# A two-stage recurrent and routed layer on one Trainium2 core: a new order of work at the changeover between its stages

## The reference

```python
xn = _layernorm(x, axis=-1)
s = recurrence(xn, A, BC)      # h = h * A + xn_t over the 2048 steps of a sequence, then h @ BC
scores = einsum('bsh,eh->bse', xn, gate_w)          # 8 experts
chosen = argmax(scores, axis=-1)
y = xn + einsum('bsh,fh->bsf', xn, expert_w[chosen])  # each token: the expert with the top score
g = silu(y)
x = x + s * g
```

## Time and profile before

| | |
|---|---|
| median of 3 runs | 529.57 us (529.09 to 530.28) |
| the profiled execution, its own time | 528.31 us |
| its span | 526.6 us |
| TensorE (matmul) busy in the span | 498.6 us, 95% |
| VectorE busy | 415.2 us, 79% |
| GpSimd busy | 317.9 us, 60% |
| ScalarE busy | 260.3 us, 49% |
| HBM traffic | 235 GB/s over the span |

### The profile page before, as it was taken

How to read it: one execution, slowest core, us unless ns; L and a number is a source line. 1 busy time by engine, 2 the same in 40 slices (tenths; PEclk the granted TensorE clock), 3 DMA queues, 4 the chain that set the end, 5 groups by cost and what they waited for, 6 DMA issues and landing times. The chain is left out here.

```text
span 526.6 us, 10784 instructions
## 1 busy us (share of the span) xinstructions
PE 498.6 (95%) x2776; PEld 391.8 (74%) x2777; DVE 415.2 (79%) x1068; ACT 260.3 (49%) x500; POOL 317.9 (60%) x358
## 2 busy tenths in 40 slices
PE   6699999999999999999987999999999999999993
PEld 6466776777777777777776888888888888887882
DVE  5979899899989998999732677777777777777773
ACT  4556676677677667767720333333333333333330
POOL 3535756766766676666644366666766666656652
PEclk9989999999999999999988999999999999999998
DMA  8995777887877787787346467776867777757720
GB/s 235 383 344 159 249 218 237 254 229 249 263 238 235 240 260 217 249 266 239 114 124 203 138 222 240 230 250 217 268 224 228 227 234 214 228 193 249 228 80 10
DMA packets 65411, 116.98 MB, mean 222 GB/s; under 512 B 8842, under 2 KB 26250, under 8 KB 65300
## 3 DMA queue, kind: packets, MB, share of 16 engines
q1 hardware_dynamic: 47328, 64.59, 39.2%
q0 software_dynamic: 18048, 52.02, 31.3%
HBM read 66.27 MB, written 57.48 MB: 235 GB/s over the span
## 5 line engine op out<-in xcount | busy, mean ns | idle before, releaser
L983 PE MATMUL ps_s<-w_hi,split 128*128 x284 | 118.8, 418 | 0.1
L596 ACT ACTIVATE ps_s<-ps_s 128x512 f32<-128x512 f32 x71 | 41.3, 582 | 154.5 <-issue 94.5
L470 POOL DMA_INDIRECT out_dram<-work x71 | 73.7, 1038 | 71.8 <-issue 45.3
L984 PE MATMUL ps_s<-w_lo,split 128*128 x284 | 112.9, 398 | 0.0
L985 PE MATMUL ps_s<-w_hi,split 128*128 x284 | 112.8, 397 | 0.0
L902 PE MATMUL ps_s<-bc_hi,split 128*128 128x512 f32 x256 | 105.3, 411 | 0.0
L903 PE MATMUL ps_s<-bc_lo,split 128*128 128x512 f32 x256 | 102.4, 400 | 0.0
L460 POOL DMA_INDIRECT work<-token_rows,work x71 | 72.6, 1023 | 31.1 <-issue 24.4
L394 POOL TENSOR_TENSOR split<-work,split 128x1024 fp32r<-128x1024 f32 x32 | 76.2, 2380 | 10.1 <-ACT split L524 9.9
L412 POOL DMA_INDIRECT slot_table<-token_id,slot_id x64 | 63.0, 985 | 26.1 <-issue 20.9
L638 DVE TENSOR_TENSOR_SCAN work<-a_col,work,ps_xt 128x256 f32<-128x256 f32 x112 | 74.3, 725 | 0.2
(11 more groups left out here) (103 smaller groups left out, 734.1 us busy)
## 6 DMA issues: line engine op xcount, KB each, us to landing
token_rows<-work SPq DMA_DIRECT2D x31, 528.0 KB, 3.1
work<-in_L_attn_inputs_dram SPq DMA_DIRECT2D x31, 512.0 KB
token_rows<-work SPq DMA_DIRECT2D x29, 512.0 KB
work<-in_L_ffn_expert_w_dram SPq DMA_DIRECT2D x128, 64.0 KB
slot_table<-w_lo SPq DMA_DIRECT2D x1, 4160.0 KB, 17.8
token_rows<-in_L_attn_inputs_dram SPq DMA_DIRECT2D x3, 512.0 KB
work<-token_rows,work POOLq DMA_INDIRECT x71
out_dram<-work POOLq DMA_INDIRECT x71
```

Of the source, the lines that this page charges most:

```text
L470: nc.gpsimd.indirect_dma_start(out=out_flat, out_offset=bass.IndirectOffsetOnAxis(ap=slot_tok[:, n:n + 1], axis=0), in_=o_sb[:, u], in_off ...
L983: nc.tensor.matmul(z_ps[v], hi, wh, start=(k == 0), stop=False)
L984: nc.tensor.matmul(z_ps[v], hi, wl, start=False, stop=False)
```

## The change

FIRST = 3 is new. What it does, by engine:

- **GpSimd.** Its last two groups are written out in another order: the id scatters of group 30 go ahead of `low_part` of group 31. Once all ids have landed it reads, in three small indirect DMAs (128 lines of 64 bytes each, `first_ids`), the ids of the first three tiles straight into `ids2`. It gathers the rows of tile 0 by them, and only then reads the whole table (`all_ids`), then gathers tiles 1 and 2 by `ids2`, and tiles 3 to 5 by `slot_tok`. The iota for `j_row` moves to the start of the kernel, with two more (`j_first`, `slot_first`).
- **TensorE.** In group 30 the ranks stand between the two `product_hi`, and `score_parts` of group 31 waits for the slots of group 30. The counts are made directly behind the ranks of group 31, by two more products with its one-hot rows, so they don't wait for GpSimd's last `seen` (whose last sum is gone). The 34 + 46 transposes are gone; 26 products of 128x512 with a block of weights (`stay_busy`) stand there, their results unused. The transpose of the ids of all tiles stands inside the products of tile 0, after the ninth of twelve. Tile 1 is turned after tile 0's products, no longer before them.
- **VectorE.** It places group 30 before it routes group 31, reads the counts between the two steps of placing group 31, and computes the slots of three tiles (`slot2`) ahead of `blk_row`. In stage 2, `low_x2` of tile 0 stands directly behind its `normalise`, then the conversion of the table, `normalise` of tile 1, the copy to `slot_tok`, `low_x2` of tile 1, `normalise` of tile 2.
- The little buffers of the plan lie in `xnt`, no longer in `work`. SyncE and ScalarE keep their order.

The diff, cut to its core:

```diff
@@ gpsimd
-            for c in range(GROUPS):
+            for c in range(GROUPS - 2):
                 group(0, c, left=GROUPS - 1 - c)
-            nc.gpsimd.iota(j_row, ...)
+            count(0, GROUPS - 2)
+            next_ids(0, GROUPS - 1)
+            scatter_ids(0, GROUPS - 2)
+            low_part(0, GROUPS - 1)
+            scatter_ids(0, GROUPS - 1)
+
             for v in range(2):
                 pool.wait_ge(id_stored[v], 32 * (GROUPS // 2))
-            pool.wait_ge(blk_row_ready, 1)
-            nc.gpsimd.indirect_dma_start(
-                out=blk_i[0:PLANNED].rearrange("p q w -> p (q w)"), out_offset=None, in_=table,
...
+            def first_ids(j):
+                pool.wait_ge(slot2_ready, 1)
+                nc.gpsimd.indirect_dma_start(
+                    out=ids2[:, j], out_offset=None, in_=table_flat,
+                    in_offset=bass.IndirectOffsetOnAxis(ap=slot2[:, j:j + 1], axis=0),
+                    bounds_check=TROWS * P - 1, oob_is_err=False).then_inc(ids2_loaded[j], 16)
+
+            def all_ids():
+                pool.wait_ge(blk_row_ready, 1)
+                pool.wait_ge(lo_done, GROUPS)
...
             def gather(it, c):
...
-                pool.wait_ge(slot_tok_ready, 1)
-                wait(pool, o_ready, n - RR + 1)
+                if n < FIRST:
+                    pool.wait_ge(ids2_loaded[n], 16)
+                    tok = ids2[:, n, 0:1]
+                else:
+                    pool.wait_ge(slot_tok_ready, 1)
+                    wait(pool, o_ready, n - RR + 1)
+                    tok = slot_tok[:, n:n + 1]
...
+            for j in range(FIRST):
+                first_ids(j)
             for v in range(2):
                 pool.wait_ge(s_stored[v], 16 * (GROUPS // 2 + (TPG - 1 if v == LAST else 0)))
-            for c in range(RR):
+            gather(0, 0)
+            all_ids()
+            for c in range(1, RR):
                 gather(0, c)
@@ vector
+                if left == 1:
+                    place(it, c, 0)
+                    place(it, c, 1)
                 if left == 0:
                     place(it, c, 0)
+                    nc.vector.tensor_scalar(tile_i[:, 0], count_ps, float(P - 1), None, ALU.add).then_inc(plan_step, 1)
                     place(it, c, 1)
...
             normalise(0, 0)
+            low_x2(0, 0)
+            dve.wait_ge(blk_loaded, 16)
+            nc.vector.tensor_copy(blk_f[0:PLANNED], blk_i[0:PLANNED, :, 0]).then_inc(blk_f_ready, 1)
             normalise(0, 1)
-            low_x2(0, 0)
+            dve.wait_ge(slot_turned, 1)
+            nc.vector.tensor_copy(slot_tok[:, :], slot_ps[:, 0:TILES]).then_inc(slot_tok_ready, 1)
+            low_x2(0, 1)
             normalise(0, 2)
-            low_x2(0, 1)
@@ tensor
+            turn_x(0, GROUPS - 1)
+            product_hi(0, GROUPS - 2, 0)
+            ranks(0, GROUPS - 2)
+            product_hi(0, GROUPS - 2, 1)
+            score_parts(0, GROUPS - 1, placed=True)
+            product_lo(0, GROUPS - 2, 0)
+            product_lo(0, GROUPS - 2, 1)
+            scores(0, GROUPS - 1)
+            ranks(0, GROUPS - 1, counted=True)
             product_hi(0, GROUPS - 1, 0)
-            pe.wait_ge(seen_ready, GROUPS)
-            pe.wait_ge(slot_ready, GROUPS)
...
             product_lo(0, GROUPS - 1, 0)
             product_hi(0, GROUPS - 1, 1)
             product_lo(0, GROUPS - 1, 1)
-            keep_warm(x2_ps[0], 34)
-            pe.wait_ge(blk_f_ready, 1)
-            nc.tensor.transpose(slot_ps[:, 0:PLANNED], blk_f[0:PLANNED], ident[0:PLANNED, 0:PLANNED]).then_inc(slot_turned, 1)
-            keep_warm(x2_ps[0], 46)
+            def stay_busy(times):
+
+                for _ in range(times):
+                    nc.tensor.matmul(x2_ps[1], w_hi[:, 0, 0:P], w_hi[:, 0], start=True, stop=True)
+
+            stay_busy(26)
...
+                    if isinstance(it, int) and it + c == 0 and k == CH - 2:
+                        turn_slots()
...
             turn_x2(0, 0)
-            for c in range(RR):
+            tile(0, 0, ahead=False)
+            turn_x2(0, 1)
+            for c in range(1, RR):
                 tile(0, c)
```

More of the change, by code:

```diff
@@ L205, in bass_recurrent_routed @@
         blk_loaded = sem("blk_loaded")
+        ids2_loaded = [sem(f"ids2_loaded{j}") for j in range(FIRST)]
         row_loaded = [sem(f"row_loaded{u}") for u in range(RR)]
@@ L766, in group @@
                     turn_w(c + 1)
-                    route(it, c + 1, left >= 3)
+                    route(it, c + 1, left >= 3, behind=left > 1)
             for c in range(GROUPS):
@@ L784, in _ @@
             step(nc.vector.tensor_tensor_scan(tile_cum[:, :], ones_f[:, :], tile_f[:, :], 0.0, ALU.mult, ALU.add), 4)
-            step(nc.vector.tensor_scalar(done[:, :], tile_cum[:, :], j_col[:, 0:1], None, ALU.is_le), 5)
+            step(nc.vector.tensor_tensor(
+                done2, tile_cum[:, :].unsqueeze(1).to_broadcast([P, FIRST, E]),
+                j_first[:, :].unsqueeze(2).to_broadcast([P, FIRST, E]), ALU.is_le), 5)
+            nc.vector.tensor_reduce(pick2[:, 0], done2, AX.X, ALU.add)
@@ new lines, in _ @@
+            step(nc.vector.tensor_tensor(done2_n, done2, tile_f[:, :].unsqueeze(1).to_broadcast([P, FIRST, E]),
+                                         ALU.mult), 6)
+            step(nc.vector.tensor_reduce(pick2[:, 1], done2_n, AX.X, ALU.add), 7)
+            step(nc.vector.scalar_tensor_tensor(pick2[:, 2], pick2[:, 0], float(TOKENS // P), pick2[:, 1], ALU.mult,
+                                                ALU.subtract), 8)
+            nc.vector.scalar_tensor_tensor(slot2, pick2[:, 2], float(P), slot_first[:, :], ALU.mult,
+                                           ALU.add).then_inc(slot2_ready, 1)
@@ L786, in _ @@
+            step(nc.vector.tensor_scalar(done[:, :], tile_cum[:, :], j_col[:, 0:1], None, ALU.is_le), 9)
             nc.vector.tensor_reduce(pick[:, 0:1], done[:, :], AX.X, ALU.add)
[L787 to L788 removed]
+            step(nc.vector.tensor_tensor(done_n[:, :], done[:, :], tile_f[:, :], ALU.mult), 10)
+            step(nc.vector.tensor_reduce(pick[:, 1:2], done_n[:, :], AX.X, ALU.add), 11)
@@ L878, in scores, with ranks @@
                 last.then_inc(score_done, 1)
-            def ranks(it, c):
+            def ranks(it, c, counted=False):
                 pe.wait_ge(onehot_ready, 4 * it + c + 1)
@@ L892, in ranks @@
                 last = nc.tensor.matmul(rank_ps, before[:, :], onehot[:, c % 2], start=False, stop=True)
+                if counted:
+                    for i in range(TPG):
+                        nc.tensor.matmul(count_ps, ones[:, :], seen[:, c % 2, i], start=(i == 0), stop=False)
+                    for i in range(TPG):
+                        last = nc.tensor.matmul(count_ps, ones[:, :], onehot[:, c % 2, i], start=False,
+                                                stop=(i == TPG - 1))
                 last.then_inc(rank_done, 1)
@@ L947, in _ @@
                     group(it, c)
-            for c in range(GROUPS - 4, GROUPS - 1):
+            for c in range(GROUPS - 4, GROUPS - 2):
                 group(0, c)
-            ranks(0, GROUPS - 1)
-            product_hi(0, GROUPS - 1, 0)
-            pe.wait_ge(seen_ready, GROUPS)
-            pe.wait_ge(slot_ready, GROUPS)
-            for i in range(TPG):
-                last = nc.tensor.matmul(count_ps, ones[:, :], seen[:, GROUPS % 2, i], start=(i == 0),
-                                        stop=(i == TPG - 1))
-            last.then_inc(count_done, 1)
+            turn_x(0, GROUPS - 1)
[7 more added lines that the diff above has]
+            ranks(0, GROUPS - 1, counted=True)
+            product_hi(0, GROUPS - 1, 0)
             product_lo(0, GROUPS - 1, 0)
@@ L974, in turn_x2, with turn_slots @@
                 last.then_inc(x2_done, 1)
+            def turn_slots():
+                pe.wait_ge(blk_f_ready, 1)
+                nc.tensor.transpose(slot_ps[:, 0:PLANNED], blk_f[0:PLANNED],
+                                    ident[0:PLANNED, 0:PLANNED]).then_inc(slot_turned, 1)
             def expert(it, c, e):
```

86 lines of the change are left out of this document (48 added, 38 removed).

## The result

| | before | changed |
|---|---|---|
| median of 5 runs, us | 529.09 (526.62 to 530.28) | 532.76 (530.83 to 534.12) |
| profiled execution, its time and span, us | 528.31, 526.6 | 530.83, 529.0 |
| TensorE's gap before the last ranks, us | 1.74 | 3.20 |
| first gather of rows | 279.11 | 278.33 |
| products of tile 0, 1, 2, 3 start | 286.94, 291.75, 294.97, 298.21 | 285.70, 293.13, 296.39, 299.63 |

The ratio is 1.007, with an interval of 1.0041 to 1.0098: 3.7 us slower. The forecast was 529.6 with a range up to 531.8, so it was wrong, and on the slow side. In short: a GpSimd instruction that the change moved now runs beside two small VectorE instructions and holds the first of them up for 1.7 us, the late last ranks then bring TensorE's clock down at a place where it delays the first gather, and a second loss that was forecast did not come.

What follows compares the result with a forecast made beforehand. TensorE was taken as the bound, busy 208.97 of 209.00 us from 291 to 500 us. A gain of 1.4 us and a clock loss of 1.5 gave +0.1 on the median 529.57: about 529.6, range 527.0 to 531.8.

Steps and rivals of the forecast that it cites:

- The last `place`: VectorE's placing of group 31, which the last id scatters need: forecast at 265.4, where it had been at 265.18.
- The stores of s: End of stage 1: they let the first gather start at 274.8 at full clock, 276.5 if the clock falls.
- G: Start of the first gather of rows: 275.0 with 276.5 as the bound, 4.1 us (2.6 us) earlier than 279.11.
- the rival "slower": Gap before the last ranks lowers the clock, late s store delays the first gather: +1.6 us, 531.2; chance 0.19.
- The small reads: Three id reads on GpSimd: the first 2.99 us behind the last scatter's start, then 1.3 us apart.
- From G to the products: From the first gather to tile 0's first products: 7.2 us, so products at 282.2, 4.7 us earlier.
- The table behind one gather: Table read queued behind tile 0's gather: lands at G + 7.3, before TensorE's ninth product wants it; no stall.
- That rival (0.05): Table lands after tile 0's ninth product, gain of G given back: +1.4 us or more, 531.0; chance 0.05.
- The gap behind tile 0: TensorE's new gap between tile 0's and tile 1's products: 3.4 us, against 0.36 us before.
- The second fall of the clock: TensorE's clock falls again in the gap behind tile 0, costing 1.5 us (bounds 0 and 1.7).
- the rival "faster": Clock stays up behind tile 0: -1.4 us, 528.2; 526.6 if tile 0 also runs partly at full clock; chance 0.35.
- the sum: Shift of the start of tile 2's products: 1.4 us gained, 1.5 lost to the clock, +0.1 us in all.

Runs made afterwards that it cites:

- experiment 3: Changed kernel, its GpSimd order kept, with `low_part` of group 31 held back until that group's one-hot rows are there: 0.9997 of the kernel before.
- experiment 2: Changed kernel with `low_part` of group 31 put back ahead of the id scatters of group 30: 0.9995 of the kernel before.
- 6: On top of experiment 2, `stay_busy(36)` for `stay_busy(26)` and `stay_busy(7)` between the turn of tile 0 and its products: 0.9976 of the kernel before.
- 7: On top of experiment 2, tiles 0 and 1 gathered ahead of the table, next tile turned inside the products of the one before: 0.9971 of the kernel before.
- experiment 8: The edits of 6 and 7 together, run twice: 0.9941 and 0.9936 of the kernel before.
- the second of 10: On top of experiment 2, product and residual of tile 0 put ahead of `normalise` of tile 3: 1.0008 of the kernel before.
- experiment 4: Changed kernel with the three new iotas moved behind the constants that all engines wait for, on their own semaphore: 1.0043 of the kernel before.

## Why the prediction was wrong, step by step

- **The last `place` at 265.4.** This is the step that failed. It read: "the ranks of group 30 add some 0.25 us to TensorE's path and the two count products with the one-hot rows 0.1, while routing group 31 without a place in its midst saves 0.2". Measured: 267.56. The instructions were counted on each engine alone, and `low_part` only as something that stands "between" two sets of scatters; nobody asked what VectorE does in those 2.4 us. Its pair took 1.67 us more; 0.34 us was there before group 30, and some 0.15 is the rest. The answer was in the trace of before, in rows that the prediction did not read. VectorE and GpSimd, at the start of that kernel:

```profile
16.64 1.57 DVE L698 SCALAR_TENSOR_TENSOR ranked<-score,top,prio 128x8 f32<-128x8 f32 x2
23.51 1.40 DVE L651 SCALAR_TENSOR_TENSOR half<-mv,half 128x2 f32<-128x2 f32 x1
```
```profile
15.58 2.40 POOL L394 TENSOR_TENSOR split<-work,split 128x1024 fp32r<-128x1024 f32 x1
22.53 2.36 POOL L394 TENSOR_TENSOR split<-work,split 128x1024 fp32r<-128x1024 f32 x1 [3.43 <-ACT split L524]
```

  The second is a small step of the statistics (`half`). Both times GpSimd's instruction ends (17.98 and 24.89) while a VectorE instruction is under way that takes 1.4 us instead of some 0.2, and that one ends 0.02 to 0.03 us later. It is no rare case: in this trace 17 of these instructions (15 of `half`, 2 of `ranked`) start beside `low_part` and end 0.02 to 0.03 us behind it, whether they had started 1.4 or 0.2 us before. The Trainium skill, "SBUF — State Buffer", section "SBUF: two separate sides", has it as a rule: a GpSimd instruction that reads SBUF and a VectorE instruction with two inputs in SBUF, and GpSimd and a VectorE instruction in a 2-port perf mode, exclude each other for the whole of the one that started first. `ranked` reads `score` and `prio`; the reductions beside it read one tensor. The trace agrees, with 2.04 against 0.36 us for the one and 0.17 for the other, and with the end of the held instruction right behind the end of `low_part`. The `tensor_scalar` of experiment 3, with one tensor input, was held in the same way (1.74 us); which mode it ran in no trace shows.
- **The stores of s and G.** G was put at 275.0, with 276.5 if the clock fell. The gap before the last ranks was 3.20 and not 1.65 us, and it fell, as in all six profiles with the pair held up. 276.5 and the 0.34 that this execution was late at group 30 and the 1.7 of the pair give 278.5; measured 278.33. Without the pair's delay the clock stayed up in six of the seven profiles of its variants that left this gap unfilled (2, 3, 6, 7, both of 8 and the second of 10; it fell in the first of 8), and in experiment 2 the gather starts 22.35 us behind group 30's scores where the forecast has 22.5. So the reasoning behind 275.0 held, on a premise that didn't. The rival "slower", whose chance was 0.19, came true in its first half: the clock fell and the store decided.
- **The small reads**: first read 2.95 us behind the last scatter's issue (2.99 taken), spacing 1.35 and 1.32 (1.3 taken). Right.
- **From G to the products**: 7.37 us (7.2 taken). Tile 0 at half clock: 4.56 us up to the turn of tile 1, 4.75 taken. Right.
- **The table behind one gather**: converted at 286.92, 8.6 us behind G, where 7.3 was taken. It was still in time: TensorE turned the ids at 289.45, without a wait. That rival (0.05) didn't happen.
- **The gap behind tile 0**: 2.87 us from the turn of tile 1 to tile 1's products; 3.4 taken. Half a us to the good.
- **The second fall of the clock** (1.5 us): the clock stood at 1.00 behind the gap, and tile 2's products came 3.26 us after tile 1's. The forecast rested on this step, and it failed too. The size was right (1.5 in the one profile that had it), the chance of it not: one profile in ten. Had everything else held, the rival "faster" would have come true, and experiment 2 is that case: its changeover is 1.5 us shorter than before's, 1.4 was worked out. Its time is level (0.9995), and the interval of that, -2.1 to +1.5 us, takes in both no gain and the whole gain of 1.5.
- **"Everything from tile 4 on is untouched."** The instructions are. Whether their time is stays open (1.5 us longer in the mean of four profiles against two, with a spread of 3.6). The time moved by 3.7 us and the start of tile 2's products by 1.4, so the sum made there did not hold the whole.
- **What was to cost nothing**: the iotas. Experiment 4 shows no cost, and could not show one of 0.3 us. SyncE's order was not varied.

So by its own mark, the start of tile 2's products, the sum was +0.1 and the trace shows +1.4. The difference of 1.3 us is 3.3 for G (0.3 from ahead of group 30, 1.7 for the pair, 1.3 for the late store), 0.2 for the way to the products, less 0.7 for tile 0 and its gap, less 1.5 for the fall that didn't come. Two errors of 1.7 and 1.3, the second following from the first, were half hidden by an error the other way: that the sum missed by no more is luck.

## What to carry to other kernels

When a step moves on one engine, list what the other engines do in its new place, and look for the same pair side by side elsewhere in the trace. An outlier in a group of equal instructions (here 1.57 us among 32 pairs with a mean of 0.43 in the kernel before) is the price of that neighbourhood. Keep large GpSimd instructions like `low_part` away from chains of small VectorE instructions that others wait for, even if that means a later start for something else (experiment 3). And look at filler and order together: a few products of filler in the waits of the changeover gave as much as a better order of the work behind the first gather. Either came out 0.2 to 0.3% below the kernel before, both together 0.6%.

## What the runs showed of the hardware

- A pair of VectorE `scalar_tensor_tensor` of 8 numbers a partition took 2.04 to 2.17 us when the first of them started beside a GpSimd `tensor_tensor` of 128x1024, and 0.36 us clear of it. The first took 1.90 to 2.03 us and ended 0.03 us behind GpSimd's. The reductions beside it kept their 0.17 to 0.22 us. A `tensor_scalar` of 8 int32 with one tensor input was held up too (1.74 against 0.16 us, one profile).
- The same gap of TensorE does not always bring the clock down. Before the last ranks, gaps of 1.74 and 1.80 us were followed by half clock in three of five profiles (the kernel before twice, the first of experiment 8; not in 6 and in the second of 10), gaps of 1.53 us in none of four, gaps of 3.20 us and more in all six, in three of them before the gap was over. The gap of some 2.8 us behind tile 0, with transposes at both its ends, was followed by it in one of ten.
- GpSimd's indirect DMA, when nothing else held it, started 1.3 us behind the one before it in all kernels, whether it moved 64 bytes or 4 KB a row.
